# Two recurrent transformer layers: constant mask rows in the stacks, sequence 1's q and k inside the first maxima, and a reordered tail

## The chip, the cores and the metric

One core of a Trainium2 chip. The time is device microseconds of one execution. Before: 641.8 us, the median of 3 runs (640.47 to 642.42).

## The reference

Eight sequences of 512 tokens with 128 features pass two layers: `x = x + s * silu(g)`, with `xn` the layer norm of `x` in each.

- Layer 0, `s`: causal attention in latent form, 16 heads of 8. With `xn`, scores are `q_lat . c_kv / sqrt(8)`, masked above the diagonal, softmax, times values. Layer 0, `g`: a mixture of 8 experts (top 2; logits are `xn . w_route` plus the cosine of the token and the centroids), each a gelu network of 64 hidden units.
- Layer 1, `s`: a normed `h` gives keys and queries of 64 and values of 128; a matrix W is updated token after token, `W = W - 0.01 * (W k - v) k^T`, read out as `W q`; `s = xn + y`. Layer 1, `g`: `xn @ sign(weight).T`.

The sequential update is solved in four chunks of 128 tokens, each with the inverse of a triangular 128x128 matrix that is built up in levels.

## The kernel before

All engines walk one written schedule (`HEAD`, then `iteration` with `FIRST_PLAN`, `PLAN`, `LAST_PLAN`). An iteration has four groups of four heads, each of ten units; a unit (step, u) can carry named pieces, and every engine executes its own part of each piece in this order. In a steady iteration a unit does three things:

- `s_unit`, for the next sequence: TensorE makes scores of queries by keys in `ps_s` (units 0 to 3: four diagonal tiles of 128 columns and the mask as one matmul of 4x128 columns, identity times `negmask`; units 4 to 9: tiles off the diagonal). VectorE takes the maximum over keys into `cand` (L1422).
- `e_unit`, for the current sequence: scores again, transposed, in `ps_e` (first the mask on the diagonal tiles, then for each tile row j one matmul over all later queries), and ScalarE takes the exponential into `prob` (L1218). The maximum is already subtracted, since it stands as rows 72 to 74 of the stack.
- the pieces: `pv` (probabilities times values, L907), the experts (`h`, `gb`, `out`), and for older sequences the second layer (`c_...`, `lev_a1` to `lev_d6`, `c_u`, `c_y`, `c_r`).

`qst` and `kst` are the stacks, two of each by parity: q and k are split in three bf16 parts, and 9 part pairs x 8 features are 72 rows (PAIRS), with three rows of maxima in q against ones in k (SROWS = 75). They are filled through DRAM: SP writes the parts to `q_scratch` and `k_scratch` (L428), loads them back in halves of eight heads (L441, L443; `stacks0`, `stacks1`), and `m_rows` sends the maxima through `max_scratch` (L449, L451). All of these stand in SP's one queue, in the schedule's order; `e_unit` waits for `mrow_loaded`.

`HEAD` works through the weights, the layer norm, q and k of sequence 0, its router and experts, then q and k of sequence 1, its stacks, gelu and constants for the masks; the iteration under `FIRST_PLAN` then has only the maxima of sequence 0, with idle matmuls (`keep_busy`) in place of `e_unit`. Six iterations run `PLAN`, a seventh has no second sequence to load, and the last runs `LAST_PLAN`: exponentials of sequence 7 beside the second layer of sequence 6, then the tail, in which the second layers of 6 and 7 are interleaved (`last:` is sequence 7).

Token norms for the cosine come from squares on ScalarE (`squares_of`, L1166) and a power on GpSimd (`token_norms`). Layer norms: VectorE's statistics, GpSimd's power of -0.5 (`ln_rstd`), VectorE's scaling (`ln_norm`; `hn_norm` and `xn2_norm` in layer 1, whose two scalings are one power over eight values, L576).

## Time and profile before

| | |
|---|---|
| median of 3 runs | 641.8 us |
| profiled execution | 642.34 us |
| its span, first to last instruction | 640.6 us |
| mean granted clock of TensorE | 0.984 of full |
| TensorE / VectorE / ScalarE / GpSimd busy | 94% / 61% / 57% / 26% |
| bytes read from and written to DRAM | 24.46 and 9.96 MB |

Busy shares are averages over stages with different limits. Matmuls overlap, so a TensorE that counts as busy need not be streaming all the time. A "releaser" is what ended an idle time.

### The profile page before, as it was taken

The numbers are of one execution on the slowest core, as the hardware profiler recorded it, in microseconds if no ns is written. First come the engines' busy times: TensorE is split into PE (matmuls) and PEld (weight loads), VectorE is DVE, ScalarE is ACT, GpSimd is POOL, SyncE is SP. The second block draws the span as 40 slices with busy tenths as digits, with TensorE's granted clock in tenths as the row PEclk, the third lists the DMA queues.
The fourth block names the chain that finished last, engine by engine and source line by source line (L and its number), as shares of the span: only waits on it lengthen the run. The fifth ranks groups of instructions, "written<-read, shape, count | busy, mean of one in ns | idle before, by whom it ended". The sixth has DMA issues, their size and how long they took to land.

```text
span 640.6 us, 16904 instructions
## 1 busy us (share of the span) xinstructions
PE 601.3 (94%) x7002; PEld 382.2 (60%) x7002; DVE 390.7 (61%) x975; ACT 363.0 (57%) x743; POOL 163.4 (26%) x310
## 2 busy tenths in 40 slices
PE   7799999899999999999999999999999998997987
PEld 3345655576565766586566756586667665553564
DVE  3369676758668576848566675857675664413432
ACT  4331467755675575746674576646674667574420
POOL 4356122313223220332223230412232202210211
PEclk9899999999999999999999999999999999899888
DMA  3665003500341013310441014210430000100001
GB/s 85 162 157 135 9 1 99 141 9 4 87 121 56 4 35 99 92 41 9 107 110 42 2 52 112 62 41 11 124 92 27 3 10 1 42 1 1 4 2 33
DMA packets 28886, 35.60 MB, mean 56 GB/s; under 512 B 3947, under 2 KB 25258, under 8 KB 27658
## 3 DMA queue, kind: packets, MB, share of 16 engines
q1 hardware_dynamic: 28778, 34.52, 21.1%
q8 instruction: 55, 0.90, 0.6%
q14 instruction: 21, 0.17, 0.1%
q10 hardware_dynamic: 32, 0.01, 0.0%
HBM read 24.46 MB, written 9.96 MB: 54 GB/s over the span
## 4 chain that ended last, share of the span: by engine, by line
PE 60%; DVE 10%; issue 4%; ACT 4%; POOL 2%; DVEq 0%; POOLq 0%
PE ps_v L907 8%; PE ps_s L888 7%; PE ps_e L873 6%; PE ps_a L833 4%; PE ps_a L819 3%; PE ps_e L870 3%; DVE cand L1422 3%; PE ps_c L972 3%; PE ps_s L891 2%; PE ps_c L954 2%; PE ps_a L790 2%; PE ps_c L1057 2%; DVE stats L1344 1%; DVE hid L1406 1%; PE ps_c L941 1%
## 5 line engine op out<-in xcount | busy, mean ns | idle before, releaser
L1422 DVE TENSOR_REDUCE cand<-ps_s 128x4 f32<-128x512 f32 (+1 forms) x320 | 212.1, 684 | 63.7 <-PE ps_s L891 44.4
L1218 ACT ACTIVATE prob<-ps_e 128x512 f32<-128x512 f32 x320 | 188.8, 598 | 100.4 <-PE ps_e L873 96.4
L888 PE MATMUL ps_s<-kst,qst 72*128 72x128 bf16 (+1 forms) x1024 | 124.7, 233 | 8.9 <-DVE cand L1422 7.1
L873 PE MATMUL ps_e<-qst,kst 75*128 75x384 bf16 (+3 forms) x512 | 122.1, 300 | 0.0
L888 PEld LDWEIGHTS ps_s<-kst,qst 72*128 72x128 bf16 x1024 | 71.4, 98 | 69.3 <-DVE cand L1422 39.5
L907 PE MATMUL ps_v<-prob,vaug 128*32 128x512 f32 (+3 forms) x1024 | 89.5, 445 | 0.0
L870 PE MATMUL ps_e<-identb,negmask 128*128 128x256 bf16 (+1 forms) x320 | 81.0, 253 | 7.2 <-ACT prob L1218 7.0
L873 PEld LDWEIGHTS ps_e<-qst,kst 75*128 75x128 bf16 x512 | 50.3, 98 | 17.8 <-issue 0.3
L891 PE MATMUL ps_s<-negmask,identb 128*128 128x512 bf16 x128 | 48.8, 381 | 0.0
L706 PE MATMUL ps_e<-identb 128*128 128x512 bf16 x116 | 42.8, 427 | 3.1 <-POOL state L501 3.1
L870 PEld LDWEIGHTS ps_e<-identb,negmask 128*128 128x128 bf16 x320 | 31.3, 98 | 18.5 <-ACT prob L1218 14.4
L907 PEld LDWEIGHTS ps_v<-prob,vaug 128*32 128x32 f32 x1024 | 23.5, 108 | 30.2 <-issue 25.4
L972 PEld LDWEIGHTS ps_c<-second 32*32 32x32 f32 x2072 | 24.9, 107 | 23.0 <-issue 16.1
L819 PE MATMUL ps_a<-xnT,w1s 128*128 128x512 f32 x64 | 34.4, 619 | 2.9 <-DVE logit L1379 2.1
L617 POOL CAST mparts<-nm 128x32 bf16<-128x32 f32 x16 | 3.3, 209 | 126.3 <-DVE nm L1429 126.3
L972 PE MATMUL ps_c<-second 32*32 32x32 f32 x2072 | 32.6, 194 | 3.0 <-DVE second L1485 2.5
L833 PE MATMUL ps_a<-w2s,hid 128*128 128x128 f32 x256 | 32.7, 281 | 0.9 <-ACT mrow L1210 0.9
L1197 ACT ACTIVATE hid<-ps_a,vecT 128x512 f32<-128x512 f32 x32 | 22.0, 687 | 20.1 <-PE ps_a L819 20.1
L833 PEld LDWEIGHTS ps_a<-w2s,hid 128*128 128x128 f32 x256 | 31.4, 192 | 1.8 <-ACT mrow L1210 1.5
L1411 DVE SCALAR_TENSOR_TENSOR gate_out<-tG,ps_a 128x512 f32<-128x512 f32 x8 | 5.5, 689 | 34.9 <-ACT tG L1205 34.9
L1205 ACT ACTIVATE tG<-ps_a 128x512 f32<-128x512 f32 x8 | 4.8, 597 | 38.4 <-PE ps_a L835 38.4
L1406 DVE TENSOR_TENSOR hid<-hid,ps_a 128x512 f32<-128x512 f32 x32 | 21.6, 677 | 4.1 <-PE ps_a L826 4.1
(336 smaller groups left out, 922.7 us busy)
## 6 DMA issues: line engine op xcount, KB each, us to landing
qst<-q_scratch SPq DMA_DIRECT2D x48, 192.0 KB
kst<-k_scratch SPq DMA_DIRECT2D x16, 576.0 KB
q_scratch<-qparts SPq DMA_DIRECT2D x24, 128.0 KB, 2.3
k_scratch<-kparts SPq DMA_DIRECT2D x24, 128.0 KB, 2.3
x_res<-in_L_attn_x_dram SPq DMA_DIRECT2D x8, 256.0 KB, 2.8
xn<-in_L_attn_x_dram SPq DMA_DIRECT2D x7, 256.0 KB, 3.3
out_dram<-second SPq DMA_DIRECT2D x7, 256.0 KB, 2.5
max_scratch<-mrow SPq DMA_DIRECT2D x16, 96.0 KB, 1.7
```

The costliest lines, as they stand in the source:

```text
L706: mm(ps_e[:, 1, :].rearrange("p (a c) -> p a c", c=P), identb[:, :], bcast(identb[:, :], 1, 4), start=True, stop=True, skip_group_check=True)
L819: mm(ps_a[:, :], w1s[:, 2 * c:2 * c + 2, :].rearrange("p e f -> p (e f)"), xnT[b.parity][:, :], start=True, stop=True)\
L833: mm(ps_a[:, tok(i)], hid[:, c, tok(i)], w2s[:, c, :], start=(i == 0 and c == 0), stop=False, skip_group_check=True)
L870: mm(diag, negmask[:, :], bcast(identb[:, :], 1, len(todo)), start=True, stop=False, skip_group_check=True)
L873: last = mm(ps_e[:, bank, at:at + TOK - P * j], k[0:SROWS, hd, tok(j)], q[0:SROWS, hd, P * j:TOK], start=False, stop=True, skip_group_chec ...
L888: last = mm(ps_s[:, bank, w * n:w * (n + 1)], q[0:PAIRS, hd, tok(i)], k[0:PAIRS, hd, keys[0]:keys[1]], start=(n == 0), stop=True, skip_gro ...
L891: last = mm(ps_s[:, bank, :].rearrange("p (a c) -> p a c", a=GH), identb[:, :], bcast(negmask[:, :], 1, GH), start=False, stop=True, skip_ ...
L907: last = mm(ps_v[32 * hh:32 * hh + 32, P * j:TOK], vaug[:, j, head_of(grp, hh), :], prob[:, u, o:o + TOK - P * j], start=(j == 0 and grp % ...
L972: last = mm(bank[SQ * col:SQ * col + SQ, SQ * i:SQ * i + SQ], lhsT(row, col, i), rhs[SQ * row:SQ * row + SQ, i, :], start=True, stop=True, ...
L1218: af(prob[:, u, :], ps_e[:, u % 2, :], ACT.Exp).then_inc(S["e_emptied"], 1)
L1406: vec.tensor_tensor(hid[:, c, :], hid[:, c, :], ps_a[:, :], ALU.mult).then_inc(S["a_emptied"], 1)
L1422: vec.tensor_reduce(cand[:, i, h0:h0 + FILLS * (len(hds) - 1) + 1:FILLS, S_SLOT[u]], ps_s[:, u % 2, :].rearrange("p (a c) -> p a c", a=len ...
```

## The change

Masks: rows 75 to 127 of the stacks (53, `MROWS`) get constants: the first rows of the identity in q, of `negmask` in k. A diagonal tile that is contracted over all 128 rows so gets the mask of its first 53 queries or keys, and the mask matmul covers the other 75 columns. In `e_unit` a tile row's matmul is cut into the diagonal tile (128 rows) and the rest (75 rows). Rows 72 to 74 of q must be zero during the maxima, so each half of a stack load also writes zeros there. The constants are built on GpSimd in `prob` and loaded into each parity once (`load_pads`).

Transfers: q's stack rows in pieces of 1024 instead of 4096 bytes, k's in three transfers without broadcast; q and k writes of sequence 0 alternate; fewer transfers for the small loads, the first expert weights on a semaphore of their own.

Order: in `HEAD` h0 and h1 come before the logits; xnt, q, k and stacks of sequence 1 move into the first maxima, as do `masks`. Token norms are computed on GpSimd from the variance and rstd. `ln_rstd` of layer 1 first makes the four values that `hn_norm` needs, then the others. `LAST_PLAN`: `pv2`, `yt`, `x1` come sooner; sequence 7's `xn2_norm`, `c_xn2t`, `c_ffn` and `c_vk` stand earlier. Some numbers of `keep_busy` matmuls differ.

```diff
-STACK_DMAS, WRITE_DMAS = 4, 6
+STACK_DMAS, WRITE_DMAS = 7, 6
 PAIRS = PARTS * PARTS * HD
 MAXROW = 96
 SROWS = PAIRS + PARTS
+MROWS = 128 - SROWS
+EVEN = 48
...
-    (2, 8): ["c_ffn"], (2, 9): ["pv1"], (3, 2): ["pv2"], (3, 4): ["yt"], (3, 6): ["pv0"], (3, 9): ["pv1"], (4, 0): ["lev_a1"],
-    (4, 1): ["lev_d1"], (4, 2): ["pv2", "lev_a2"], (4, 3): ["yt", "x1", "last:ln2_stats", "lev_d2", "fill4", "last:ln2_rstd", "lev_a3", "last:hn_norm", "fill6"],
-    (4, 4): ["last:c_ht", "lev_d3", "fill2", "last:c_kt", "last:c_qt", "lev_a4", "fill1"],
-    (4, 5): ["last:c_gram", "lev_d4", "turned0", "low_blocks", "turned1", "last:c_vk", "fill1", "lev_a5", "fill2"],
-    (4, 6): ["last:lev_a1", "lev_d5", "fill1", "last:lev_d1", "lev_a6", "fill1", "last:xn2_norm"], (4, 7): ["last:lev_a2", "lev_d6", "fill1", "last:lev_d2", "c_u0", "fill1"],
-    (4, 8): ["last:lev_a3", "c_y0", "fill1", "last:lev_d3", "c_r1", "fill1"], (4, 9): ["last:lev_a4", "c_u1", "fill1", "last:lev_d4", "last:turned0", "last:low_blocks", "last:turned1", "c_y1", "fill1"],
-    (5, 0): ["last:c_xn2t", "c_r2", "fill1", "last:lev_a5", "c_u2", "last:c_ffn"], (5, 1): ["last:lev_d5", "prev:c_y2", "fill1", "last:lev_a6", "prev:c_r3", "fill1"],
-    (5, 2): ["last:lev_d6", "prev:c_u3", "prev:c_y3", "fill1", "last:c_u0", "prev:c_out", "fill1", "last:c_y0"],
-    (5, 4): ["last:c_r1", "fill1", "last:c_u1", "fill1", "last:c_y1"], (5, 5): ["last:c_r2", "fill1", "last:c_u2", "fill1", "last:c_y2"],
+    (2, 8): ["c_ffn"], (2, 9): ["pv1"], (3, 2): ["pv2"], (3, 4): ["yt"], (3, 6): ["pv0"], (3, 9): ["pv1"], (4, 0): ["pv2", "lev_a1", "fill2"],
+    (4, 1): ["yt", "x1", "last:ln2_stats", "lev_d1", "fill8", "lev_a2", "fill4", "last:ln2_rstd", "lev_d2", "fill2", "last:hn_norm", "lev_a3", "fill2"],
+    (4, 3): ["last:c_ht", "last:xn2_norm", "fill2", "last:c_kt", "last:c_qt", "lev_d3", "fill1", "last:c_vk", "last:c_gram", "lev_a4", "fill1"],
+    (4, 4): ["lev_d4", "last:c_xn2t", "lev_a5", "turned0", "low_blocks", "turned1", "fill1", "last:lev_a1", "last:c_ffn", "fill1", "last:lev_d1", "lev_d5", "fill1"],
+    (4, 5): ["last:lev_a2", "lev_a6", "fill1", "last:lev_d2", "lev_d6", "fill1", "last:lev_a3", "c_u0", "fill1"], (4, 6): ["last:lev_d3", "c_y0", "fill1"],
+    (4, 7): ["last:lev_a4", "c_r1", "fill1", "last:lev_d4", "c_u1", "fill1"], (4, 8): ["last:lev_a5", "last:turned0", "last:low_blocks", "last:turned1", "c_y1", "fill1"],
+    (4, 9): ["last:lev_d5", "c_r2", "fill1", "c_u2", "last:lev_a6"], (5, 0): ["prev:c_y2", "fill1", "last:lev_d6", "prev:c_r3", "fill1"],
+    (5, 2): ["last:c_u0", "prev:c_u3", "fill1", "last:c_y0", "prev:c_y3", "fill1"],
+    (5, 4): ["last:c_r1", "fill1", "prev:c_out", "last:c_u1", "fill1", "last:c_y1"], (5, 5): ["last:c_r2", "fill1", "last:c_u2", "fill1", "last:c_y2"],
...
-HEAD = [("weights", None), ("ln1_stats", 0), ("ln1_rstd", 0), ("centroids", None), ("ln1_norm", 0), ("ln1_stats", 1), ("ln1_rstd", 1),
-        ("xnt", 0), ("weight_k", None), ("q", 0), ("k", 0), ("stacks0", 0), ("stacks1", 0), ("rn_first", 0), ("constants", None),
-        ("late_loads", None), ("prepare", None), ("logits", 0), ("ln1_norm", 1), ("h0", 0), ("gates", 0), ("h1", 0), ("gate_norm", 0), ("h2", 0),
-        ("h3", 0), ("xnt", 1), ("q", 1), ("k", 1), ("stacks0", 1), ("stacks1", 1), ("gelu", 0), ("masks", None), ("busy", None)]
+HEAD = [("weights", None), ("ln1_stats", 0), ("ln1_rstd", 0), ("rn_first", 0), ("centroids", None), ("ln1_norm", 0), ("ln1_stats", 1), ("ln1_rstd", 1),
+        ("xnt", 0), ("weight_k", None), ("q", 0), ("k", 0), ("stacks0", 0), ("stacks1", 0), ("constants", None), ("late_loads", None),
+        ("prepare", None), ("h0", 0), ("h1", 0), ("logits", 0), ("h2", 0), ("gates", 0), ("ln1_norm", 1), ("h3", 0), ("gate_norm", 0),
+        ("gelu", 0), ("busy", None)]
 FIRST_PLAN = {
-    (0, 1): ["gt"], (0, 7): ["prepare2"], (0, 9): ["prepare3"], (1, 1): ["prepare4"],
-    (2, 0): ["m_parts0"], (2, 4): ["m_rows0"], (2, 5): ["masks2"], (3, 2): ["v"], (4, 0): ["m_parts1"],
+    (0, 0): ["xnt"], (0, 2): ["q"], (0, 4): ["k", "stacks0", "stacks1"], (0, 7): ["gt"], (1, 2): ["masks"], (1, 6): ["prepare2"], (1, 9): ["prepare3"],
+    (2, 0): ["m_parts0"], (2, 2): ["prepare4"], (2, 4): ["m_rows0"], (2, 5): ["masks2"], (3, 2): ["v"], (4, 0): ["m_parts1"],
 }
...
-    yield from iteration(None, seqs[0], None, None, None, plan=FIRST_PLAN)
+    yield from iteration(seqs[1], seqs[0], None, None, None, plan=FIRST_PLAN)
...
+        q_pad, k_pad = (prob[0:MROWS, 0, 256 * n:256 * n + 256].bitcast(BF16) for n in range(2))
...
+            def load_pads(p):
+
+                few = MROWS - EVEN
+                sp.wait_ge(S["pad_ready"], 2)
+                for st, pad in ((qst[p], q_pad), (kst[p], k_pad)):
+                    sp.dma_start(st[SROWS + few:P, :, :], bcast(pad[few:MROWS, :], 1, HEADS)).then_inc(S[f"pads_loaded{p}"], 16)
+                    sp.dma_start(st[SROWS:SROWS + few, :, :], bcast(pad[0:few, :], 1, HEADS)).then_inc(S[f"pads_loaded{p}"], 16)
+                sp.wait_ge(S["ones_ready"], 1)
+                sp.dma_start(kst[p][PAIRS:SROWS, :, :], bcast(ones_bf[:, :], 1, HEADS)).then_inc(S[f"pads_loaded{p}"], 16)
...
+            sp.dma_start(w1s[:, :, :], w1_in.rearrange("e d f -> d e f")).then_inc(S["expert_loaded"], 16)
+            load_pads(0)
...
+                if b.c == 0 and n == 0:
+                    return
+                tensors = (0, 1) if b.c == 0 else (n,)
                 for r, ready in enumerate(("hi_ready", "mid_ready", "parts_ready")):
-                    sp.wait_ge(S[ready], b.count(2, n + 1))
-                    to = (q_scratch[b.parity][:, r], k_scratch[b.parity][r])[n]
-                    sp.dma_start(to.rearrange("d h q -> h d q"), parts[n][:, r, :]).then_inc(S["scratch_written"], 16)
+                    for t in tensors:
+                        sp.wait_ge(S[ready], b.count(2, t + 1))
+                        to = (q_scratch[b.parity][:, r], k_scratch[b.parity][r])[t]
+                        sp.dma_start(to.rearrange("d h q -> h d q"), parts[t][:, r, :]).then_inc(S["scratch_written"], 16)
...
-                                 max_dma_last_dim=4096).then_inc(loaded, 16)
-                sp.dma_start(kst[b.parity][0:PAIRS, heads, :].rearrange("p h q -> p (h q)"), bcast(k_rows, 1, PARTS)).then_inc(loaded, 16)
+                                 max_dma_last_dim=1024).then_inc(loaded, 16)
+                sp.dma_start(qst[b.parity][PAIRS:SROWS, heads, :], bcast(zeros_bf[:, :], 1, HALF_HEADS)).then_inc(loaded, 16)
+                for r in range(PARTS):
+                    sp.dma_start(kst[b.parity][r:PAIRS:PARTS, heads, :].rearrange("p h q -> p (h q)"), k_rows,
+                                 max_dma_last_dim=1024).then_inc(loaded, 16)
...
+            for pad, of in ((q_pad, identb), (k_pad, negmask)):
+                g.tensor_copy(pad.rearrange("p (i c) -> p i c", c=P), bcast(of[0:MROWS, :], 1, NT)).then_inc(S["pad_ready"], 1)
...
-                g.tensor_scalar(r.vare[n][:, 0, :], variance, LN_EPS, None, ALU.add).then_inc(r.S[f"var{n}"], 1)
                 if n == 0:
+                    g.tensor_scalar(r.vare[n][:, 0, :], variance, LN_EPS, None, ALU.add).then_inc(S["var0"], 1)
                     pool.wait_ge(S["var0"], o.count(1, 1))
                     g.tensor_tensor(r.rstd[n][:, 0, :], r.vare[n][:, 0, :], halfpow[:, 0, :], ALU.pow).then_inc(S["rstd0"], 1)
+                    pool.wait_ge(S["rstd0"], o.count(1, 1))
+                    g.tensor_tensor(ss[:, :], variance, r.rstd[n][:, 0, :], ALU.mult).then_inc(S["ss_ready"], 1)
+                    pool.wait_ge(S["ss_ready"], o.count(2, 1))
+                    g.tensor_tensor(ss[:, :], ss[:, :], r.rstd[n][:, 0, :], ALU.mult).then_inc(S["ss_ready"], 1)
                 else:
                     g.tensor_scalar(r.vare[n][:, 1, :], variance, 1 + LN_EPS, LN_EPS * LN_EPS, ALU.mult, ALU.add).then_inc(r.S["var1"], 1)
+                    pool.wait_ge(r.S["var1"], o.count(2, 1))
+                    g.tensor_tensor(r.rstd[n][:, 1, :], r.vare[n][:, 1, :], halfpow[:, 0, :], ALU.pow).then_inc(r.S["rstd1"], 1)
+                    g.tensor_scalar(r.vare[n][:, 0, :], variance, LN_EPS, None, ALU.add).then_inc(r.S["var1"], 1)
                     pool.wait_ge(r.S["var1"], o.count(2, 2))
-                    g.tensor_tensor(r.rstd[n][:, :, :], r.vare[n][:, :, :], halfpow[:, :, :], ALU.pow).then_inc(r.S["rstd1"], 1)
+                    g.tensor_tensor(r.rstd[n][:, 0, :], r.vare[n][:, 0, :], halfpow[:, 0, :], ALU.pow).then_inc(r.S["rstd1"], 1)
...
-                    diag = ps_e[:, bank, 0:P].rearrange("p (a c) -> p a c", a=1)
+                    diag = ps_e[:, bank, MROWS:P].rearrange("p (a c) -> p a c", a=1)
                 else:
                     step = 384 if u < 8 else 256
-                    diag = ps_e[:, bank, :].rearrange("p (a c) -> p a c", c=P)[:, 0:step // P + 1:step // P, :]
-                mm(diag, negmask[:, :], bcast(identb[:, :], 1, len(todo)), start=True, stop=False, skip_group_check=True)
+                    diag = ps_e[:, bank, :].rearrange("p (a c) -> p a c", c=P)[:, 0:step // P + 1:step // P, MROWS:P]
+                mm(diag, negmask[:, :], bcast(identb[:, MROWS:P], 1, len(todo)), start=True, stop=False, skip_group_check=True)
                 for hh, j, at in todo:
                     hd = head_of(grp, hh)
-                    last = mm(ps_e[:, bank, at:at + TOK - P * j], k[0:SROWS, hd, tok(j)], q[0:SROWS, hd, P * j:TOK],
+                    last = mm(ps_e[:, bank, at:at + P], k[:, hd, tok(j)], q[:, hd, tok(j)],
                               start=False, stop=True, skip_group_check=True)
+                    if j < NT - 1:
+                        last = mm(ps_e[:, bank, at + P:at + TOK - P * j], k[0:SROWS, hd, tok(j)], q[0:SROWS, hd, P * (j + 1):TOK],
+                                  start=False, stop=True, skip_group_check=True)
...
+                if b.c < 2 and grp == 0 and u == 0:
+                    pe.wait_ge(S[f"pads_loaded{b.parity}"], 80)
+                rows = P if u < NT else PAIRS
                 for n, hh in enumerate(hds):
                     w = keys[1] - keys[0]
                     hd = head_of(grp, hh)
-                    last = mm(ps_s[:, bank, w * n:w * (n + 1)], q[0:PAIRS, hd, tok(i)], k[0:PAIRS, hd, keys[0]:keys[1]],
+                    last = mm(ps_s[:, bank, w * n:w * (n + 1)], q[0:rows, hd, tok(i)], k[0:rows, hd, keys[0]:keys[1]],
                               start=(n == 0), stop=True, skip_group_check=True)
                 if u < NT:
-                    last = mm(ps_s[:, bank, :].rearrange("p (a c) -> p a c", a=GH), identb[:, :], bcast(negmask[:, :], 1, GH),
+                    last = mm(ps_s[:, bank, :].rearrange("p (a c) -> p a c", a=GH)[:, :, MROWS:P], identb[:, :],
+                              bcast(negmask[:, MROWS:P], 1, GH),
...
-            def squares_of(b):
-                after(act, S["rn_ready"], b.count(1, 0))
-                for i in range(NT):
-                    af(tG[:, i * P:(i + 1) * P], x_tile(b)[:, i, :], ACT.Square, accum_out=ss[:, i:i + 1]).then_inc(S["ss_ready"], 1)
```

Left out: GpSimd's setup in another order (identity first; `negmask`, a row block of zeros and the pads before the rest), `token_norms` reading `ss` scaled by 128, and the changed numbers of `keep_busy`.

## Rows read from the trace of the kernel before

**Rows 1.** The page: busy time, share of the span and instructions of each engine.

```profile
PE 601.3 (94%) x7002; PEld 382.2 (60%) x7002; DVE 390.7 (61%) x975; ACT 363.0 (57%) x743; POOL 163.4 (26%) x310
```

**Rows 2.** Windows by stage: PE, PEld, DVE, ACT, POOL busy, clock, DMA share, GB/s.

```profile
0.00:36.04 36.04, 27.93 (x91) 12.27 (x92) 11.88 (x51) 14.70 (x42) 15.57 (x40) 0.95 0.53 131
...
36.04:65.40 29.36, 28.96 (x216) 14.94 (x215) 25.60 (x43) 6.55 (x16) 15.42 (x45) 1.00 0.57 133
...
65.40:121.00 55.60, 53.20 (x481) 32.05 (x478) 38.02 (x82) 36.42 (x67) 11.46 (x26) 1.00 0.22 56
...
262.40:333.20 70.80, 68.63 (x859) 45.65 (x858) 47.93 (x121) 44.55 (x91) 18.35 (x32) 1.00 0.23 61
...
542.80:584.70 41.90, 38.02 (x310) 21.51 (x314) 10.62 (x29) 28.26 (x55) 8.52 (x13) 0.96 0.06 16
...
584.70:640.60 55.90, 45.80 (x795) 30.05 (x787) 22.52 (x71) 12.76 (x38) 9.42 (x11) 0.88 0.04 11
```

**Rows 3.** Windows, two stretches inside one steady stage.

```profile
261.60:273.40 11.80, 10.27 (x87) 5.77 (x85) 11.73 (x30) 7.19 (x13) 5.39 (x8) 1.00 0.14 39
...
296.00:304.30 8.30, 8.24 (x195) 5.46 (x194) 8.16 (x26) 6.03 (x15) 2.14 (x6) 1.00 0.05 16
```

**Rows 4.** TensorE instructions in order of time, one unit: start, length, line, operation.

```profile
275.48 0.39 PE L888 MATMUL ps_s<-kst,qst 72*128 72x128 bf16 x4
275.71 0.38 PE L891 MATMUL ps_s<-negmask,identb 128*128 128x512 bf16 x1
275.93 0.22 PE L870 MATMUL ps_e<-identb,negmask 128*128 128x128 bf16 x1
275.98 0.38 PE L873 MATMUL ps_e<-qst,kst 75*128 75x512 bf16 x1
```

**Rows 5.** Groups by line and shape: busy us, mean ns, idle before.

```profile
L870 PE MATMUL ps_e<-identb,negmask 128*128 128x256 bf16 x192 | 53.0, 276 | 1.4 <-ACT prob L1218 1.4
...
L891 PE MATMUL ps_s<-negmask,identb 128*128 128x512 bf16 x128 | 48.8, 381 | 0.0
...
L873 PEld LDWEIGHTS ps_e<-qst,kst 75*128 75x128 bf16 x512 | 50.3, 98 | 17.8 <-issue 0.3
```

**Rows 6.** Transfers issued by SP, in order of time.

```profile
54.73 0.34 SPq L449 DMA_DIRECT2D max_scratch<-mrow  x1
...
59.98 0.24 SPq L451 DMA_DIRECT2D qst<-max_scratch  x1
...
243.84 1.13 SPq L441 DMA_DIRECT2D qst<-q_scratch  x3
```

**Rows 7.** VectorE instructions in order of time.

```profile
260.52 0.69 DVE L1422 TENSOR_REDUCE cand<-ps_s 128x4 f32<-128x512 f32 x1
...
587.02 0.69 DVE L1435 COPY yT<-ps_v 128x512 f32<-128x512 f32 x1
...
594.42 1.11 DVE L1359 TENSOR_SCALAR qst<-x,last_mv,last_rstd 128x128 f32<-128x128 f32 x4 [1.85 <-POOL last_rstd L576]
```

**Rows 8.** TensorE in order of time, in the start and in the tail.

```profile
28.78 0.66 PE L778 MATMUL ps_a<-ident,att 128*128 128x128 f32 x4 [0.78 <-ACT hid L1197]
...
613.76 0.45 PE L972 MATMUL ps_s<-qst 32*32 32x32 f32 x32
...
616.87 0.44 PE L972 MATMUL ps_s<-qst 32*32 32x32 f32 x16 [0.30 <-ACT kst L1229]
...
620.03 0.81 PE L972 MATMUL ps_s<-qst 32*32 32x32 f32 x24 [1.41 <-DVE kst L1512]
```

**Rows 9.** Windows, the first maxima while the stacks are loaded.

```profile
42.00:60.00 18.00, 17.96 (x137) 9.34 (x136) 15.99 (x26) 1.86 (x7) 6.67 (x26) 1.00 0.64 138
```

**Rows 10.** GpSimd's powers in order of time: four values, then eight.

```profile
5.47 1.04 POOL L572 TENSOR_TENSOR rstd<-vare,halfpow 128x4 f32<-128x4 f32 x1
...
592.72 1.67 POOL L576 TENSOR_TENSOR last_rstd<-last_vare,halfpow 128x8 f32<-128x8 f32 x1
```

**Rows 11.** Windows, a stretch of the tail.

```profile
620.20:630.40 10.20, 9.82 (x62) 6.93 (x59) 2.84 (x8) 0.90 (x3) 3.93 (x4) 0.50 0.00 0
```

73 lines of the change are left out of this document (36 added, 37 removed).

## The prediction

> **What bounds the kernel now.** I read the page first, then busy time by stage, then one steady stage cut into stretches, then single matmuls in order of time, and last the start and the tail.
>
> TensorE is busy for 601.3 of 640.6 us [rows 1]. "Busy" overstates it, since matmuls overlap, so look at the stages [rows 2]: the start to the first maximum (36.0 us), the maxima of sequence 0 (29.4), then seven stages that put the maxima of one sequence beside the exponentials of another (55.6, five of 70.8, and one of 68.0, which together end at 542.8), the exponentials of sequence 7 alone (41.9), and the tail (55.9). In a steady stage TensorE is busy for 68.6 of 70.8 us, VectorE for 47.9 and ScalarE for 44.6: TensorE sets the pace on average. But in two stretches of that stage VectorE is busy for 11.73 of 11.80 us and for 8.16 of 8.30 [rows 3]. There the maxima and the work between them set the pace, and a shorter matmul only makes TensorE wait. 20.1 of 70.8 us are such, so what is saved on TensorE comes through for about two thirds. In the first maxima VectorE has 25.6 of 29.4 us, one reduction after another (40 in that time, 0.73 us each); in the last exponentials stage nobody is full.
>
> **The mask part.** For the spacing of matmuls, look at start times, not at durations [rows 4]. The four S matmuls of 128 columns start within 275.48 to 275.71, so 0.057 us each; the S mask of 512 columns holds the engine from 275.71 to 275.93, 0.22; the E mask of 128 columns 0.05. All of it is about 0.43 ns per column, at a granted clock of 1.00.
>
> S: each of 128 masks [rows 5] shrinks from 4 x 128 to 4 x 75 columns: 212 x 0.43 = 0.09 us, times 16 per sequence = 1.45 us per stage. E: 64 diagonal tiles per sequence lose 53 columns each, in 16 masks of one tile and 24 of two (192 over the run [rows 5]): 64 x 53 x 0.43 = 1.45 us. Against that the E matmul of tiles 0 to 2 is cut in two (48 more weight loads and matmuls per sequence, columns in all the same). What a cut costs no row shows; the distance from column time is 2 to 3 ns in these rows, so 0.1 us per stage. Below: 0, the load hides completely. Above: a weight load is recorded with 98 ns [rows 5], against 55 for the 128 columns before it: 43 ns x 48 = 2.1 us. I take 0.1, since the four S matmuls each bring such a load and still start 0.057 apart. A mask of 75 columns is shorter than any bf16 matmul here; if loads need the 55 ns, 16 x 0.02 = 0.35 us is lost. The contraction over 128 rows instead of 72 or 75 I price at nothing: the identity masks already use 128 rows and have the same price per column.
>
> Sum per stage: 1.45 + 1.45 - 0.1 = 2.8 us on TensorE. About 0.9 of it lies in VectorE's two stretches (groups 0 and 2, most units of each). Of the other 1.9 I take 1.6 as real, because the second layer's chains go TensorE to ScalarE to TensorE and TensorE waits a little more. Six stages of 1.6 and the first (55.6 us, fewer other pieces, so more of it is back-to-back maxima) with 1.3: **10.9 us**. Bounds: 0.5 per stage (3.5) and all of it (19.6).
>
> The Trainium skill, "TensorE: Matmul & The Clock Gate", section "Back-to-back issue gap", speaks against the cut: in a stream of load and matmul pairs it gives about 81 ns per matmul of 128 columns, so 48 more pairs would cost far more than I allow. By that figure a stage would pay 48 x 28 ns = 1.3 us more, and the seven stages about 6 us of gain less. This trace has 0.057 us for just such pairs, and the measurement decides.
>
> Squares for the token norms leave ScalarE; two small GpSimd operations replace them behind the rstd. In the body both lie under TensorE: nothing.
>
> **Stack loads.** Each half issues seven transfers instead of four (q in 1 KB pieces, k in three, a zero row block). Three q issues take 1.13 us of SP's time at 243.84 [rows 6]; the half is needed 16.7 us later, when the next stage's maxima begin at 260.52 [rows 7]. Seven at 0.4 to 0.8 us are 3 to 6 us, so they are hidden: nothing. Queued behind them on SP are only m_rows1, the residual and the next x. If the cover went, each us late would cost a us in each stage.
>
> **The start.** Before, sequence 1's transposes, q and k stand between sequence 0's feed-forward and the maxima: from 28.78 [rows 8] to the first maximum at 36.04, 7.3 us. They move into the first maxima. Then the stack load is what comes last. Its issue time hardly moves: SP now passes five pad transfers and their wait on GpSimd (pads built behind two more memsets), but the parts are the later event; q and k writes alternate, about 1 us saved. I expect the first maximum at about 28.5. The moved work costs in the first maxima: two subtractions over 128x512 out of PSUM, which I price like a reduction of that size, 0.69 us [rows 7], plus waits because q passes TensorE, ScalarE, VectorE while only a few reductions are there to cover: 2.5 to 3 us. So the maxima would end 7.5 - 2.7 = 4.8 us sooner.
>
> What is late next is the queue of transfers. In order after 21 us: stacks of sequence 0 (2.3 MB), late weights 0.3, the second pads (2 x 53 rows x 16 KB = 1.7), parts 0.8, stacks of sequence 1 (2.3), together 7.4 MB. The first exponential also waits for m_rows0, whose second transfer is issued only when the first has landed: before, at 59.98 against 54.73 for the first [rows 6], i.e. behind the stacks. In 42 to 60 us the engines moved 138 GB/s at a share of 0.64 [rows 9], so 216 at a full share. 7.4 MB at 180 to 216 GB/s from 21 us end at 55 to 62, plus two landings of about 2 us that the queue cannot cover, so the exponentials start at 60 to 66 instead of 65.4. I take 62.3: **3.1 us** won, bounds 0 and 5.
>
> **Last exponentials (41.9 us).** Only the E masks: 1.3 us on TensorE, but ScalarE and TensorE alternate there. The first layer-norm power before hn_norm takes four values, not eight. I take **1 us**; bounds 0 and 2.
>
> **The tail.** (a) pv2 moves ahead of the level pieces, so VectorE's copy of yT, 587.02 before [rows 7], starts about 1.3 us sooner. (b) The rstd chain: eight-value power 1.67 us [rows 10], four-value power 1.04 [rows 10], one tensor_scalar less before it: 0.9 us. Of these 2.2 us part is taken back, since lev_d2 of sequence 6 now stands in front of hn_norm on VectorE: hn_norm, 594.42 before, at about 593.2. (c) c_xn2t and c_ffn of sequence 7 move ahead. Before, lev_d4 starts at 613.76, lev_a5 at 616.87, released by c_xn2t's copy, and lev_d5 at 620.03, released by c_ffn's product [rows 8]: 6.3 us from d4 to d5. Now lev_a5 can follow d4 after about 1.3 us and d5 after 2.5, so 3.8 less. The same work must fit in earlier, where TensorE is full (PE groups of sequences 6 and 7 interleave): 1.5 us back, and xn2_norm 1.1 on VectorE. From this: about 1.2 + 3.8 - 2 = 3.0. (d) Before, 620.2 to 630.4 ran at a granted clock of 0.50, the 1.2 GHz level [rows 11], after a stretch in which TensorE waited. With the wait gone part of it may go; busy there 9.8 us, worth up to 4. I count 1. Tail: **4 us**; bounds 0 and 8.
>
> Sum: 3.1 + 10.9 + 1 + 4 = 19 us from the profiled execution's 642.3 (span 640.6 and 1.7 around it), so 623.3. The median, 641.8, is 0.5 lower: I say **623**.
>
> **Rivals.**
> - *The gain stays behind VectorE.* Stretches of 99% load grow once TensorE is faster, as rows 3 let one fear; against it, VectorE has 23 us spare per stage. 0.5 instead of 1.6 per stage: 623 + 7 = 630 (to 634). Chance 0.19.
> - *A floor per weight load.* 98 ns per pair rather than 55: E loses 2.1 us per stage and gains 1.1 to 1.45, only S remains: about 0.6 per stage, 1 us less in each of seven, and 630. Against it the 0.057 us spacing. Chance 0.08. The skill's 81 ns lies between.
> - *More comes through*: full mask saving and no clock drop in the tail, 607 to 614. For it: 1.9 us lie outside VectorE's stretches for certain. Chance 0.14.
> - *The start and the tail give nothing* (transfers of the pads, the earlier gate work in the way): 623 + 7 = 630. Chance 0.04.
> - *Slower: SP's issues.* If 1 KB pieces make an issue four times as long (1.5 us for q, 3 for k), the seven take 14 us and the half lands about 4 us late at the start of every stage: 7 x 4 = 28, so 651. It decides from 2.7 us late per stage, where seven stages eat the 19. Nothing speaks for it but that no such piece size is loaded here before. Chance 0.03.
>
> My forecast (616 to 628 by its own terms) has 0.52. The range that leaves out two in ten is 611 to 633. A measurement here cannot tell less than 0.3%, 2 us, from no change: faster 0.95, same 0.02, slower 0.03.
>
> **What would show it.** The spacing of the 75-column masks (33 or 55 ns; S masks 0.13 us), the cut matmuls starting 55 ns apart; stage length near 69.2; VectorE still full in the same stretches; first maximum near 28.5 and first exponential near 62, released by m_rows; hn_norm near 1.2 us sooner relative to the last exponential; lev_d5 of sequence 7 within 3 us of lev_d4; less of the slow clock after it. Wrong would be: a stage at 70.8 (VectorE or chains), maxima that wait for a stack load, or a longer start.

## The result and the profile after

Five runs of the changed kernel gave 647.5 us (median) and six of the one before 640.5, ratio 1.009 [1.007, 1.012]. A sixth execution of the changed kernel, at a mean granted clock of 0.555, took 905.6 us and is in no comparison. A second comparison, with ten and thirteen runs, gave 645.0 against 642.4, ratio 1.003 [1.001, 1.006]. So the change made the kernel a little slower, by 0.3 to 0.9%, where 623 us was forecast. The profile below is an execution of the second comparison: span 644.3 us.

The page of the changed kernel, busy time by engine; TensorE has 20 us less to do than before [rows 1], VectorE as much:

```profile
PE 581.6 (90%) x7385; PEld 393.3 (61%) x7385; DVE 390.9 (61%) x975; ACT 352.5 (55%) x679; POOL 172.0 (27%) x337
```

Its windows by stage, with the columns of [rows 2]: the start to the first row maximum, from there to the first exponential, and a steady stage.

```profile
0.00:39.23 39.23, 23.97 (x74) 10.75 (x75) 10.56 (x48) 10.54 (x23) 14.80 (x43) 0.83 0.75 137
39.23:84.37 45.14, 30.73 (x225) 16.46 (x224) 27.40 (x45) 8.51 (x19) 19.99 (x53) 0.87 0.80 148
277.04:346.34 69.30, 66.32 (x907) 47.05 (x906) 47.85 (x122) 43.26 (x84) 19.37 (x35) 1.00 0.27 62
```

A steady stage takes 69.3 us instead of 70.8: as forecast. But the first exponential comes at 84.4 us instead of 65.4. What the change wins behind that point, it has lost by then. In the stretch before it TensorE is busy for 30.7 of 45.1 us and the DMA engines at a share of 0.80.

What holds the start is read from SP's issues, in order of time (start, length of the issue, what is moved); `prob` is the tile in which GpSimd built the pads:

```profile
7.24 2.87 SPq L411 DMA_DIRECT2D kst<-prob  x1
...
13.22 2.70 SPq L414 DMA_DIRECT2D kst<-ones_bf  x1
...
23.42 0.60 SPq L448 DMA_DIRECT2D q_scratch<-qparts  x1
...
29.03 1.20 SPq L462 DMA_DIRECT2D qst<-q_scratch  x3
...
44.34 3.06 SPq L411 DMA_DIRECT2D kst<-prob  x1
...
50.45 2.67 SPq L414 DMA_DIRECT2D kst<-ones_bf  x1
53.17 4.33 SPq L448 DMA_DIRECT2D q_scratch<-qparts  x3
...
73.60 0.50 SPq L473 DMA_DIRECT2D max_scratch<-mrow  x1
81.32 0.26 SPq L475 DMA_DIRECT2D qst<-max_scratch  x1
```

The issues of the k pads and of the row of ones last 2.7 to 3.1 us each, where those of the two q pads before them last 0.75 and 0.91 and most small loads 0.25 to 0.6. The length isn't that of the transfer: the ones are 48 KB, and without pads in front of them (run 3) their issue takes 0.93 us. So I read it as SP waiting until the queue takes more. The small loads behind them are issued by 23.4, the parts are written from there on, and the stacks of sequence 0 are issued at 29.0; before the change the same issue stood at 20.6. The second set holds SP from 42.7 to 53.1, and sequence 1's parts and stacks come behind it. The last of the stacks is issued at 73.6; m_rows0 follows, and its second transfer at 81.3.

TensorE in order of time shows who waits for this: first for the small loads, then for the stack of sequence 1, then for the maxima's row.

```profile
25.68 0.27 PE L761 MATMUL ps_c<-ident,vecs 8*128 8x8 f32 x1 [11.87 <-DMA vkrow<-in_L_attn_bk_dram]
```

```profile
74.00 0.58 PE L925 MATMUL ps_s<-kst,qst 128*128 128x128 bf16 x4 [3.17 <-DMA kst<-k_scratch]
...
83.66 0.25 PE L901 MATMUL ps_e<-identb,negmask 128*128 128x75 bf16 x1 [8.82 <-DMA qst<-max_scratch]
```

ScalarE has its first exponential behind that, after 15.7 us without work:

```profile
84.37 0.60 ACT L1247 ACTIVATE prob<-ps_e 128x512 f32<-128x512 f32 x1 [15.71 <-PE ps_e L907]
```

### The profile page after: what moved, and what is told of

Same layout as the page of the kernel before. It is cut to its first block, busy times and chain, and to the rows that moved or that the text cites. A ratio compares the mean times of both kernels' runs of the same rounds, so it can differ in the third digit from the quotient of the medians.

```text
span 903.9 us, 17696 instructions
## 1 busy us (share of the span) xinstructions
PE 885.7 (98%) x7385; PEld 559.3 (62%) x7385; DVE 400.4 (44%) x975; ACT 361.7 (40%) x679; POOL 171.9 (19%) x337
## 4 chain that ended last, share of the span: by engine, by line
PE 94%; DVE 3%; SPq 2%; ACT 1%; issue 0%; POOL 0%; DMA 0%; POOLq 0%; DVEq 0%
PE ps_v L945 14%; PE ps_s L925 13%; PE ps_e L907 8%; PE ps_a L850 6%; PE ps_a L864 5%; PE ps_e L904 5%; PE ps_e L738 4%; PE ps_c L1010 4%; PE ps_e L901 3%; PE ps_s L928 3%; PE ps_a L819 3%; PE ps_c L992 2%; PE ps_a L828 1%; PE ps_c L1095 1%; PE ps_c L1070 1%; PE ps_v L955 1%
## 5 line engine op out<-in xcount | busy, mean ns | idle before, releaser
L925 PE MATMUL ps_s<-kst,qst 128*128 128x128 bf16 (+2 forms) x1024 | 176.9, 304 | 0.9 <-DVE cand L1453 0.5
L925 PEld LDWEIGHTS ps_s<-kst,qst 72*128 72x128 bf16 (+1 forms) x1024 | 97.8, 119 | 98.4 <-issue 51.3
L904 PE MATMUL ps_e<-qst,kst 128*128 128x128 bf16 x512 | 141.8, 297 | 0.0
L907 PE MATMUL ps_e<-qst,kst 75*128 75x256 bf16 (+2 forms) x384 | 139.5, 381 | 0.0
L945 PE MATMUL ps_v<-prob,vaug 128*32 128x512 f32 (+3 forms) x1024 | 136.7, 649 | 0.0
L901 PE MATMUL ps_e<-identb,negmask 128*128 128x150 bf16 (+1 forms) x320 | 90.7, 284 | 0.8 <-ACT prob L1247 0.7
L904 PEld LDWEIGHTS ps_e<-qst,kst 128*128 128x128 bf16 x512 | 63.4, 124 | 22.3 <-issue 1.2
L850 PE MATMUL ps_a<-xnT,w1s 128*128 128x512 f32 x64 | 55.7, 983 | 1.3 <-ACT hid L1226 0.8
L864 PE MATMUL ps_a<-w2s,hid 128*128 128x128 f32 x256 | 53.4, 384 | 0.3 <-ACT mrow L1239 0.3
L928 PE MATMUL ps_s<-negmask,identb 128*128 128x300 bf16 x128 | 53.3, 416 | 0.0
L1010 PEld LDWEIGHTS ps_c<-second 32*32 32x32 f32 x2072 | 29.8, 124 | 30.6 <-issue 28.1
```

Of the source, the lines that this page charges most:

```text
L850: mm(ps_a[:, :], w1s[:, 2 * c:2 * c + 2, :].rearrange("p e f -> p (e f)"), xnT[b.parity][:, :], start=True, stop=True)\
L864: mm(ps_a[:, tok(i)], hid[:, c, tok(i)], w2s[:, c, :], start=(i == 0 and c == 0), stop=False, skip_group_check=True)
L901: mm(diag, negmask[:, :], bcast(identb[:, MROWS:P], 1, len(todo)), start=True, stop=False, skip_group_check=True)
L904: last = mm(ps_e[:, bank, at:at + P], k[:, hd, tok(j)], q[:, hd, tok(j)], start=False, stop=True, skip_group_check=True)
L907: last = mm(ps_e[:, bank, at + P:at + TOK - P * j], k[0:SROWS, hd, tok(j)], q[0:SROWS, hd, P * (j + 1):TOK], start=False, stop=True, skip_ ...
L925: last = mm(ps_s[:, bank, w * n:w * (n + 1)], q[0:rows, hd, tok(i)], k[0:rows, hd, keys[0]:keys[1]], start=(n == 0), stop=True, skip_group ...
```

## Experiments

In all of them "the changed kernel" is the kernel after the change. Runs 1 to 4, 5 to 8 and 9 to 12 were each measured beside the kernel before, which took 642.4, 642.5 and 641.3 us; ratios are to it. "By the spans" compares one profiled execution of each kernel, which a difference in the start can shift by 2 us (see run 8).

**1. The changed kernel again.**

> The changed kernel once more, for a profile at the full granted clock. Theory Q (queue): the pad transfers fill SP's queue, the five issues take up to 3 us each, the small loads behind them land near 20 us, and TensorE stands still in the start for about 9 us; the masks themselves save 1.3 to 1.9 us per steady stage as forecast. Then the first maximum is at 37 to 38 us and a steady stage has 69 us. Theory C (clock): the start is not late by much, but TensorE gets the lower clock in more stretches of the body; then a steady stage has 71 us or more and stretches at 0.5 stand in it. Time in both: 645 to 648.

Measured: 645.0 us, ratio 1.003 [1.001, 1.006]. The trace is the one shown above: the first maximum at 39.2 us, 11.9 us of idle TensorE in front of 25.7, a steady stage of 69.3. Theory Q, with a start that is 1 to 2 us later still. It is the base of the next three.

**2. The mask matmuls of before in the changed kernel**, the pads still loaded but read by nobody.

```diff
-rows = P if u < NT else PAIRS          # and 75-column masks, cut E matmuls
+rows = PAIRS                           # 512-column S mask, 128-column E masks, E matmul in one
```

> Both kinds of mask as before (full mask matmuls over all columns, 72 and 75 rows, E matmul not cut); pads still loaded, though unused. Theory Q: slower than the changed kernel by what the masks save, 9 to 13 us, so 655 to 660, with the same late start. Theory C: the 128-row matmuls cost the clock, so this one is as fast as the changed kernel or faster, 640 to 646.

Measured: 659.2 us, ratio 1.025 [1.017, 1.034]; steady stages are back at 70.7 us: theory Q. TensorE's program still waits for the pads, but the trace puts its long waits in the start down to the small loads (13.9 us), sequence 1's stack (1.6) and the maxima's row (9.2), not to them. The masks win 14 us by the medians, 11 by the spans (655.4 to 644.3).

**3. The same without the four pad transfers of each parity.** The row of ones is still loaded.

```diff
-for st, pad in ((qst[p], q_pad), (kst[p], k_pad)):
-    sp.dma_start(st[SROWS + few:P, :, :], ...)
-    sp.dma_start(st[SROWS:SROWS + few, :, :], ...)
```

> As e1, and the four pad transfers of each parity are gone too. Theory Q: the small loads land by 15 us, the first maximum comes at 28 to 30 us, and the whole is 8 to 12 us faster than e1: 645 to 650. Theory C: the pads are hidden and this equals e1 within 2 us.

Measured: 632.1 us, ratio 0.984 [0.979, 0.990]. The eight transfers cost 27 us by the medians and 23.6 by the spans (655.4 to 631.8), in a kernel that doesn't even use them. The first maximum comes at 28.1 instead of 38.8 us, the first exponential at 63.4 instead of 83.0. Theory Q in kind, but its size was missed by more than half: it allowed 8 to 12 us, for the first maximum alone, and left out that the second set stands ahead of sequence 1's stacks. Run 7 takes the two sets apart.

**4. The last iteration's plan of before.**

```diff
-LAST_PLAN = { ... (4, 0): ["pv2", "lev_a1", "fill2"], ... }
+LAST_PLAN = { ... (4, 0): ["lev_a1"], ... }                # the table before the change
```

> The changed kernel with the old order of the last iteration (LAST_PLAN). If the new tail saves the 4 us that were forecast, this is 3 to 5 us slower than the changed kernel, about 650. If the tail's clock or order spoiled it (rival), it is equal or faster: 640 to 646.

Measured: 651.2 us, ratio 1.013 [1.007, 1.018]. By the medians the new plan wins 6 us, by the spans (648.0 to 644.3) 3.7, and of that only 0.5 lies behind the last row maximum; in the rest the two starts differ, which the plan doesn't touch. So this pair sizes the plan badly, and run 11 does it again on a quieter base.

**5. The pads kept and used, but loaded when the queue is idle.** In run 3's trace the DMA share between 70 and 90 us is 0.01 to 0.05. The pads get tiles of their own (`prob` is in use by then), sequences 0 and 1 use the masks of before, the other six the constant rows.

```diff
-q_pad, k_pad = (prob[0:MROWS, 0, ...].bitcast(BF16) for n in range(2))
+q_pad, k_pad = (sb(name, [MROWS, TOK], BF16) for name in ("q_pad", "k_pad"))
 def load_x(b):
     ...
+    if b.c == 2:
+        load_pads(0)
 def m_rows(b, half):
     ...
+    if (b.c, half) == (0, 1):
+        load_pads(1)
-rows = P if u < NT else PAIRS
+rows = P if u < NT and b.c >= 2 else PAIRS     # the E masks and cuts likewise
```

> The changed kernel with the pad rows kept, but in tiles of their own and loaded later: the four pad transfers of parity 0 are issued behind the load of sequence 2's x (about 61 us), those of parity 1 behind sequence 0's second row maxima (about 76 us), where the trace of the run without pads shows a DMA share of 0.01 to 0.05; the first two sequences use the mask matmuls of before, the six others the constant rows. Theory A, that the pads cost time only because they stand in the queue in front of the start's loads: the start is that of the run without pads (632.1 us), the stages from sequence 2 on take 69.4 instead of 70.7 us, so 632 less 9 to 11, about 622 us, ratio about 0.968. Rival B, that the pads cost wherever they are, since they hold SP for about 12 us per parity and the transfers behind them: the row maxima's transfers come late and the exponentials with them, and 628 to 636 us results. Rival C, that the masks' saving seen so far (14 us by medians) belongs to the start and not to the stages: 630 us.

Measured: 622.6 us, ratio 0.970 [0.965, 0.974]; theory A. It is the fastest kernel of the study together with run 9, 3% below the kernel before. SP's issues of the first set in it, and the windows of the start and of the 12 us in which that set moves:

```profile
58.57 0.65 SPq L411 DMA_DIRECT2D qst<-q_pad  x1
...
60.11 3.79 SPq L411 DMA_DIRECT2D kst<-k_pad  x1
64.33 2.29 SPq L412 DMA_DIRECT2D kst<-k_pad  x1
```

```profile
0.00:21.00 21.00, 16.38 (x57) 7.20 (x57) 10.09 (x44) 8.05 (x20) 14.00 (x39) 1.00 0.47 122
21.00:61.20 40.20, 36.07 (x240) 19.09 (x241) 27.84 (x49) 10.96 (x24) 19.18 (x52) 0.96 0.74 156
61.00:73.00 12.00, 11.55 (x109) 6.95 (x108) 9.94 (x16) 7.45 (x13) 2.22 (x6) 1.00 1.08 129
```

The pads are as slow here as at the start: issues of 3.8 and 2.3 us, 129 GB/s at a share of 1.08, so 12 us and more in which the queue does nothing else. But nothing waits behind them. In the windows of the changed kernel, the same two stretches:

```profile
0.00:21.00 21.00, 11.87 (x33) 5.21 (x33) 5.60 (x23) 5.38 (x12) 13.67 (x39) 0.92 0.81 127
21.00:84.40 63.40, 42.86 (x264) 22.04 (x265) 32.36 (x70) 13.70 (x30) 21.12 (x57) 0.82 0.77 149
```

Rate times time gives what is moved before the first exponential: 8.8 MB in the kernel with late pads, 12.1 MB in the changed one. The 3.3 MB between them are close to the two sets (1.7 MB each). The mean rate up to there is nearly the same in both, 145 and 143 GB/s, so the time goes with the bytes: the first exponentials are 84.4 - 61.2 = 23.2 us apart. There is a second way to be late in this, SP's own wait at each issue. No run issues the pads from another engine, so what that wait adds to the transfers' own time isn't shown.

**6. The first set issued behind the small loads.**

```diff
-load_pads(0)
 sp.wait_ge(S["small_zeroed"], 1)
 for dst, src in zero_loads + loads:
     sp.dma_start(dst, src).then_inc(S["loaded"], 16)
+load_pads(0)
```

> The changed kernel with the first five pad transfers issued behind the small loads (vectors, second weights, value and key rows) instead of in front of them; nothing is left out. Theory A, that the transfers' volume fills the start: the small loads' wait (11.9 us of idle TensorE before 25.7 us) goes, but the parts and the stacks still stand behind the pads, the first maximum stays at 37 to 40 us, and the time is 641 to 646 us. Rival B, that the order alone cost, since the preparation waits for the small loads: the first maximum comes at 30 us or so and the time is 633 to 637 us.

Measured: 645.0 us, ratio 1.004 [1.001, 1.007], as without the edit (645.0). The small loads are now issued by 10.1 us instead of 23.4 and their wait is gone, yet the first maximum stays at 39.3 and the first exponential comes at 86.6. TensorE now waits the longer for the stack:

```profile
38.31 0.61 PE L925 MATMUL ps_s<-kst,qst 128*128 128x128 bf16 x4 [12.98 <-DMA kst<-k_scratch]
```

Whether the pads stand before or behind the small loads isn't the cause; that they pass ahead of the stacks is.

**7. Only the second set loaded**, with the masks of before (between runs 2 and 3).

```diff
-for st, pad in ((qst[p], q_pad), (kst[p], k_pad)):
+for st, pad in ((qst[p], q_pad), (kst[p], k_pad)) if p else ():
```

> The changed kernel with the mask matmuls of before and without the four pad transfers of parity 0 (its ones are loaded); those of parity 1 stay where they are, behind the late weights. The same with both sets took 659 us, with neither 632 us. Theory A, that both sets cost, the first by the late first maximum (38.8 against 28.1 us), the second by sequence 1's stacks and the first row maxima, which stand behind them: about 10 to 12 us come back, 646 to 649 us. Rival B, that only the first set costs and the second is hidden: 632 to 635 us. Rival C, that only the second costs, since the first maxima of sequence 0 end into a wait for row maxima anyway: 656 to 659 us.

Measured: 647.3 us, ratio 1.008 [1.004, 1.012]: theory A. Of the 27 us between runs 2 and 3 the first set has 12 and the second 15 by the medians; by the spans (655.4, 643.7, 631.8) each has 12. Its windows to the first maximum and on to the first exponential at 72.4:

```profile
0.00:29.86 29.86, 20.69 (x73) 9.26 (x74) 10.84 (x49) 12.27 (x23) 15.14 (x43) 0.97 0.56 126
29.86:72.36 42.50, 33.70 (x224) 17.79 (x223) 27.72 (x45) 6.86 (x18) 20.07 (x53) 0.90 0.76 152
```

In the three kernels that differ in nothing but the sets, the first exponential comes at 63.4 us with none ahead of it, at 72.4 with one and at 83.0 with two. With what the following stage adds, a set of 1.7 MB costs about 12 us by the spans.

**8. The stack loads of before** in run 3's kernel.

```diff
-for s in range(PARTS): ... q_rows, max_dma_last_dim=1024
-sp.dma_start(qst[b.parity][PAIRS:SROWS, heads, :], bcast(zeros_bf[:, :], 1, HALF_HEADS))
-for r in range(PARTS): ... k_rows, max_dma_last_dim=1024
+for s in range(PARTS): ... q_rows, max_dma_last_dim=4096
+sp.dma_start(kst[b.parity][0:PAIRS, heads, :]..., bcast(k_rows, 1, PARTS))
```

> The kernel with the mask matmuls of before and no pads (632.1 us), with the stack loads as before the change too: per half three loads of 4096-element pieces and one broadcast instead of seven loads in 1024-element pieces. Theory A (the prediction's step), that the extra issues of SP cost nothing: 631 to 633 us. Rival B, that the seven issues hold the queue at the start, where the row maxima's second transfer was issued 7 us behind the stacks: 626 to 630 us. Rival C, that the smaller pieces move faster: 634 to 638 us without them.

Measured: 628.7 us, ratio 0.979 [0.975, 0.984], 3.4 us less than run 3 with intervals that overlap; by the spans 2.1. The number lies in rival B's range. 1.8 of the 2.1 lie ahead of the second maxima (61.6 against 63.3 us), half of them ahead of the first. The steady stages are equal to 0.1 us. Look at the granted clock before believing rival B: in run 3's execution it is at the 1.2 GHz level in more of the first maxima.

```profile
26.00:34.00 8.00, 7.07 (x33) 4.27 (x34) 2.08 (x3) 1.37 (x3) 0.00 (x0) 0.57 0.88 163
```

```profile
26.00:34.00 8.00, 7.22 (x38) 4.06 (x39) 3.83 (x6) 1.64 (x3) 0.91 (x2) 0.79 0.73 165
```

The first line is run 3 (clock 0.57), the second this run (0.79). The kernel of run 5, with seven issues, has 0.79 there too and its second maxima at 61.1 us.

**9. The same edit on the kernel with late pads**, with one load of zeros kept.

> The kernel with late pads (622.6 us) with the stack loads of before the change again, and one load of zeros beside them: five per half instead of seven, in pieces of 4096 elements. Without pads the same edit took the time from 632.1 to 628.7 us. Theory A, that it is the seven issues at the start that cost: 3 us less again, 619 to 620.5 us. Rival B, that the two effects share their cover: 622 to 623 us.

Measured: 621.3 us, ratio 0.968 [0.965, 0.971], against 0.970 [0.965, 0.974]; the spans are 620.0 and 619.8. 621.3 lies between the two ranges, but the traces are alike: second maxima at 61.3 and 61.1 us, the clock at 0.79 from 26 to 34 us in both. Here the form of the stack loads makes no difference (rival B), so run 8's 3 us are no price of the seven issues. Runs 5 and 12 have the same program up to 61 us and show 0.79 and 0.57 in that stretch, so the clock there differs between executions without an edit. That it is what parts run 8 from run 3 fits, but wasn't tested by itself. Run 9 also keeps the zeros that run 8 drops.

**10. The pads in pieces of 4 KB.** They are built four heads wide and moved with a quarter of the pieces.

```diff
-sp.dma_start(st[SROWS + few:P, :, :], bcast(pad[few:MROWS, :], 1, HEADS))
+sp.dma_start(wide(st[SROWS + few:P, :, :]), bcast(pad[few:MROWS, :], 1, HEADS // 4))
```

> The changed kernel with its pads where they are, but built four heads wide, so that their transfers go in pieces of 4 KB instead of 1 KB (the same bytes, a quarter of the pieces); their build on POOL grows by some 2 us each and may delay the first of them as much. Nothing is left out. In the kernel with late pads, two of the four moved 1.7 MB per parity at 129 GB/s and a DMA share of 1.08. Theory A, that a piece has a price of its own: the pads go at 180 GB/s or more, and of the 24 us that they cost a third or more comes back, 632 to 638 us. Rival B, that the price is per byte, or at the writing side: 643 to 649 us.

Measured: 645.9 us, ratio 1.007 [1.004, 1.009]: no gain, rival B. The pads are issued 2.6 us later (8.05 instead of 5.49, for the longer build) and the issues of the k pads last 2.76 and 2.77 us, much as before (2.87 and 3.02). The price isn't one of the pieces. Whether it goes with the bytes, or with the 53 partitions that are read and written, run 13 tells.

**11. The plan of before for the last iteration, with late pads.**

> The kernel with late pads (622.6 us) with the last iteration's plan as before the change. In the changed kernel the same edit cost 6.2 us by the medians, but only 0.4 to 1 us of it lay behind the last row maxima in the two profiled executions, the rest in the start. Theory A (the prediction's step: pv2 and yt earlier 1.3, c_xn2t and c_ffn earlier 1.8): 625 to 629 us. Rival B, that the difference was the start's: 622 to 624 us.

Measured: 624.2 us, ratio 0.975 [0.969, 0.980], so the plan is worth 1.6 us by the medians, which were measured beside different runs of the kernel before, and 3.2 by the ratios and by the spans (623.0 to 619.8), of which 2.7 lie behind the last exponentials. The median falls between the two ranges and the intervals overlap; the traces speak for theory A. TensorE in order of time, the last levels of sequence 7: with the plan of before and with the new one.

```profile
599.82 0.72 PE L1022 MATMUL ps_s<-qst 32*32 32x32 f32 x32
...
606.35 0.59 PE L1022 MATMUL ps_s<-qst 32*32 32x32 f32 x24 [1.41 <-DVE kst L1555]
```

```profile
600.57 0.45 PE L1022 MATMUL ps_s<-qst 32*32 32x32 f32 x32
...
602.81 0.59 PE L1022 MATMUL ps_s<-qst 32*32 32x32 f32 x24
```

The waits behind lev_d4 that [rows 8] shows are back with the old plan (6.5 us from d4 to d5) and gone with the new one (2.2).

**12. The row maxima's masks of before, with late pads.** The exponentials' masks stay changed.

```diff
-rows = P if u < NT and b.c >= 2 else PAIRS
-cut = 0 if b.c < 2 else MROWS
+rows = PAIRS
+cut = 0
```

> The kernel with late pads (622.6 us) with the row maxima's masks as before the change in all sequences (the masks of the exponentials stay changed). The masks' saving in a steady stage was 1.45 us of 70.8 where TensorE lost 2.8 us of work. Theory A, that TensorE and VectorE share the stages' limit, so that each kind of mask gives about half: 0.7 us per stage, 4 to 5 us in all, 626.5 to 628 us. Rival B, that the row maxima wait for VectorE anyway and only the exponentials' masks count: 622 to 623.5 us. Rival C, that only the maxima's masks count: 630 to 632 us.

Measured: 629.2 us, ratio 0.980 [0.976, 0.984]. One steady stage in this kernel and in the one with late pads:

```profile
257.97:328.16 70.19, 67.70 (x907) 47.05 (x906) 47.90 (x122) 43.38 (x83) 19.40 (x35) 1.00 0.26 63
```

```profile
253.93:323.21 69.28, 66.30 (x907) 47.05 (x906) 47.85 (x121) 43.27 (x84) 19.40 (x35) 1.00 0.26 64
```

TensorE is busy 1.4 us longer, as forecast for the S masks; 0.9 us of it shows in the stage, where VectorE and ScalarE do the same in both. The E masks have the other 0.5 of some 1.4. From sequence 2's first row maximum to sequence 7's last it makes 5.3 us; that the medians are 6.7 apart and the spans 8.8 has to do with the start, which is 2.4 us later in this execution and which the edit doesn't reach (its clock is 0.57 from 26 to 34 us, as in run 3, and not 0.79). The median lies outside all three ranges. By the stages it is theory A, with more for S than for E.

**13. The transfers alone.** A kernel of SP's transfers only, in eight groups of four, each group waited for before the next; its output is a copy of the input. It was executed once.

```diff
+go([(t[80:128, :, :], bcast(src[5:53, 0:W], HEADS)) for t in tiles])        # as the pads go
+go([(t[40:88, :, :], bcast(src[5:53, 0:W], HEADS)) for t in tiles])
+go([(t[0:48, :, :], bcast(src[5:53, 0:W], HEADS)) for t in tiles])
+go([(t[40:88, :, :], bcast(src[40:88, 0:W], HEADS)) for t in tiles])
+...
```

> Transfers alone, the rest of the work left out (the output is a copy of the input). Eight groups one after the other, each of four transfers of 768 KB (48 rows of 16 KB, the shape of a large pad transfer; in the last group 128 rows of 6 KB): from partitions 5 to 52 to partitions 80 to 127, as the pads go; to 40 to 87; to 0 to 47; from 40 to 87 to 40 to 87; to 80 to 127 in pieces of 4 KB; from DRAM to 80 to 127 and to 40 to 87; from and to all 128 partitions. In the kernels the pads moved at 129 GB/s. Theory A, that the destination limits them, 48 neighbouring partitions in the upper half: the first group has about 129 GB/s (6 us per transfer), 40 to 87 a third more or better, and all 128 partitions 200 GB/s or more. Theory B, that reading the same piece from SBUF sixteen times limits them: the four groups within SBUF are equal at about 129, and DRAM to the same rows is faster. Theory C, that the engines give no more for pieces of 1 KB: all groups with such pieces are within 15% of each other, the 4 KB pieces faster.

Windows within the groups, in their order (the second group falls into two stretches; columns: GpSimd busy, clock, DMA share, GB/s):

```profile
4.00:25.00 21.00, 0.00 (x0) 1.00 1.07 143
29.00:40.00 11.00, 0.00 (x0) 1.00 0.92 188
40.00:51.00 11.00, 0.00 (x0) 1.00 0.52 97
53.00:75.00 22.00, 0.00 (x0) 1.00 1.02 140
78.00:92.00 14.00, 0.00 (x0) 1.00 0.92 218
94.00:116.00 22.00, 0.00 (x0) 1.00 0.98 141
119.00:141.00 22.00, 0.00 (x0) 1.00 1.02 142
144.00:157.00 13.00, 0.00 (x0) 1.00 0.96 236
160.00:170.00 10.00, 0.00 (x0) 1.00 0.95 314
```

No theory alone. From the first issue to the last landing the eight groups take 25.5, 23.6, 25.7, 15.9, 24.7, 25.7, 15.7 and 11.0 us. Theory A missed its own test: with 5 to 52 as the source, 40 to 87 as the destination is hardly faster than 80 to 127: 23.6 us instead of 25.5 (188 GB/s first, 97 after that, 142 over both windows). But 40 to 87 takes 218 GB/s from 40 to 87 and 236 from DRAM, so in that group it was the side that is read that set the rate. And 80 to 127 takes 142 from DRAM as well, so there the side that is written is enough. Theory B fails by that, and theory C by 218 against 143 for pieces of 1 KB; pieces of 4 KB give 141. All 128 partitions take 314. So the rate goes by which partitions a transfer touches at either end, and the DMA share doesn't show it: it is 1.02 at 142 and 0.95 at 314 GB/s. For 0 to 47 as a destination the run shows nothing, since its source was 5 to 52.

The Trainium skill, "SBUF — State Buffer", section "Door 1: The DMA port swizzle (why `[64,N]` ≈ `[32,N]`)", says that partitions 0 to 63 share one half of 16 ports and 64 to 127 the other, with partitions 32 apart on the same port. By that rule 80 to 127 lie on eight ports, four of them with eight rows and four with four, and 40 to 87 on twelve ports with four rows each. These runs agree in the order of the rates, if the fullest port at either end decides; the factor between the two is 1.5 to 1.7 here and not 2.

## Why the prediction was wrong, step by step

**The step that failed is the start: "Its issue time hardly moves: SP now passes five pad transfers and their wait on GpSimd ..., but the parts are the later event".** The stacks are issued at 29.0 us instead of 20.6. The parts were not the later event, because the five transfers take SP from 5.5 to 15.9 us, and the small loads and the parts' writes come behind. I priced the wait on GpSimd and not the queue: an issue costs 0.3 to 0.9 us only while the queue has room. Run 3 shows what the start is without them: first maximum 28.1 us, where 28.5 was forecast. Run 6 shows that it doesn't help to let the small loads pass first, since the first set's 1.7 MB still come ahead of the stacks; run 5 shows what does.

**The same volume is missing in the sum of the queue.** The prediction counted 7.4 MB from 21 us on, with the second set and without the first, at "180 to 216 GB/s", which came from scaling 138 GB/s by the share of 0.64 [rows 9]. Such scaling does not hold: at a share of 0.80 the changed kernel moved 148 GB/s (its windows above), at 1.08 the pads alone moved 129, and run 13 has full shares at anything from 140 to 314. In the changed kernel 9.4 MB went from 21 us to the first exponential, at 149 GB/s, and that is 63.4 us. So 2.0 MB were missing in the sum (13 us at that rate), and the 7.4 that it had take 50 us instead of the 34 to 41 that it allowed. 149 GB/s could have been read from the trace before the change, from 21 to 65.4 us:

```profile
21.00:65.40 44.40, 41.88 (x260) 19.87 (x259) 28.31 (x54) 13.97 (x33) 19.11 (x52) 0.98 0.64 149
```

Up to the first exponential the mean rate is 145 and 141 GB/s in runs 5 and 7 too, with no set and with one. The prediction's own bound, that the start gives nothing, stood at 65.4 us; the start in truth lost 19.

**What followed from it.** TensorE was busy for 0.8 of the 9 us from 74 to 83 us, and from there to 89 us its granted clock was still 0.50, so that the first matmuls of the exponentials ran at the 1.2 GHz level. The rival "the start and the tail give nothing (transfers of the pads ... in the way)" named the mechanism but bounded it at 7 us, with a chance of 0.04; it was 19 us at the first exponential, and the pads cost 27 us by the medians between runs 2 and 3. The other slow rival, SP's issues in the steady stages, did not come: the seven issues of a half take 4.4 us, and runs 5 and 9 have equal spans with seven and with five.

**What was right, by the kernel with late pads.** Its time, 622.6 us, is the forecast's 623. That it is so close is in part luck, since it is another kernel (two sequences keep the old masks) and its terms miss in both directions, as the list shows:

- *Masks.* In the changed kernel one S unit and a pair of E units, TensorE in order of time:

```profile
38.61 0.39 PE L925 MATMUL ps_s<-kst,qst 128*128 128x128 bf16 x4
38.83 0.29 PE L928 MATMUL ps_s<-negmask,identb 128*128 128x300 bf16 x1
38.96 0.38 PE L738 MATMUL ps_e<-identb 128*128 128x512 bf16 x1
```

```profile
89.67 0.23 PE L901 MATMUL ps_e<-identb,negmask 128*128 128x150 bf16 x1
89.74 0.22 PE L904 MATMUL ps_e<-qst,kst 128*128 128x128 bf16 x1
89.79 0.27 PE L907 MATMUL ps_e<-qst,kst 75*128 75x256 bf16 x1
89.90 0.22 PE L904 MATMUL ps_e<-qst,kst 128*128 128x128 bf16 x1
```

  The S mask holds the engine for 0.13 us (38.83 to 38.96), two masks of 75 columns for 0.07, and the cut matmuls of 128 columns for 0.05 to 0.06. There is no floor per weight load, as forecast from [rows 4]; the Trainium skill's 81 ns ("TensorE: Matmul & The Clock Gate", section "Back-to-back issue gap") are not met here either. In a steady stage TensorE is busy for 66.3 instead of 68.6 us (2.3 less, 2.8 forecast), and about 1.45 come through, where 1.6 was taken. VectorE's two full stretches of [rows 3] are still there, in the changed kernel:

```profile
278.10:290.50 12.40, 10.65 (x100) 6.25 (x98) 11.61 (x30) 7.89 (x14) 6.67 (x10) 1.00 0.21 56
311.50:320.00 8.50, 8.25 (x207) 5.85 (x204) 8.05 (x26) 6.28 (x13) 2.54 (x8) 1.00 0.05 14
```

  They keep the rest. Follow one row maximum, the last of the first stretch, before and in the changed kernel:

```profile
272.70 0.68 DVE L1422 TENSOR_REDUCE cand<-ps_s 128x4 f32<-128x512 f32 x1
```

```profile
289.05 0.69 DVE L1453 TENSOR_REDUCE cand<-ps_s 128x4 f32<-128x512 f32 x1
```

  It stands 12.18 us behind the stage's first maximum before (260.52) and 12.01 after (277.04), so only 0.17 us is won there. The second stretch wins 0.11, and the other 1.2 of the 1.5 us lie outside the two, as the prediction argued.

- *Q and k inside the first maxima.* From the first maximum of sequence 0 to the end of its last it is 28.8 us before, 32.1 in the changed kernel and 33.9 in the one with late pads: 3.3 and 5.0 more, where 2.7 was taken.
- *The start without pads.* The first maximum comes at 26.8 us (9.2 sooner; 7.5 was taken) and waits 2.1 us for the stack, so the stack load does come last. Less the 5.0, the maxima end 4.2 us sooner, and 4.8 was forecast. The first exponential, at 61.2 us, follows them at once (62.3 forecast), 4.2 sooner than before; 3.1 was taken, because the queue was expected to hold it. In this kernel it doesn't: `m_rows0`'s second transfer is issued at 57.3, and no wait for a transfer stands in front of the first `ps_e` matmul. The time was right there and the reason wasn't.
- *The tail.* VectorE's first norm of sequence 7 stands 10.3 us behind the start of ScalarE's last group of exponentials:

```profile
593.38 1.76 ACT L1247 ACTIVATE prob<-ps_e 128x512 f32<-128x512 f32 x3 [0.80 <-PE ps_e L904]
```

```profile
603.70 2.10 DVE L1390 TENSOR_SCALAR qst<-x,last_mv,last_rstd 128x128 f32<-128x128 f32 x8
```

  The last group before the change:

```profile
582.91 1.79 ACT L1218 ACTIVATE prob<-ps_e 128x512 f32<-128x512 f32 x3 [0.83 <-PE ps_e L873]
```

  Before it was 11.5 (594.42 [rows 7] less 582.91), so 1.2 sooner, as forecast. With the plan of before but the new order of the powers it is 10.5: 1.0 of it is the powers'. From that norm to lev_d5 it is 23.5 us instead of 25.6, 2.1 less, where 1.8 was taken. Behind lev_d5 it is 17.0 instead of 20.6 us, since the stretch at a clock of 0.50 [rows 11] is gone; I counted 1 for it, it was 3.6. But it is gone in run 11 too, with the plan of before (the last 16 us there run at a clock of 1.00), so the waits in front of it were not what brought it, or not alone. That stays open. Executions of the kernel before differ among themselves, from 639.0 us at a mean clock of 0.995 to 645.7 at 0.981, so part of the 3.6 may be the execution's.

Against the kernel before, the spans add up: 3.7 at the start of sequence 2's maxima, 7.2 in five steady stages (1.3 to 1.5 each) and 1.8 in the last one, 8.1 behind the last row maximum with the last exponentials' masks and the tail; 640.6 - 619.8 = 20.8 us, where the forecast had 19. Term by term: start 3.7 (3.1 forecast), masks 9.0 in six stages (10.9 in seven), last exponentials and tail 8.1 (5). The tail's surplus, most of it the clock, makes up for the stage without new masks.

## What to carry to other kernels

Constant data that is loaded only once still has to pass through the queue, and a start that already waits for transfers pays for each megabyte in full: here a set of 1.7 MB cost about 12 us with the small loads behind it or in front of it, and no cost of it shows when it was moved to a time with an idle queue. Sum the bytes ahead of the first dependent instruction, those issued before the stretch that one looks at too, and take the rate from a stretch of the same trace in which the same partitions are filled, not one scaled up by the share. An SP issue's length in a quiet trace is no price for it in a full queue. And when two executions of nearly the same kernel differ by 2 us, compare the granted clock of the same stretch before giving the difference to the edit.

## What the runs showed of the hardware

The issue of a pad transfer on SP took 0.65 to 0.9 us for the first two in most runs and 2.3 to 3.8 for the next ones, at the start and in an idle queue alike; in run 7 the second of them already took 3.6 and the next two 1.1 and 2.0. A load of 48 KB took 2.7 us behind them and 0.93 alone. It isn't the bytes under way alone that make the issue wait: in run 13 four transfers of the same 768 KB from DRAM, in pieces of 16 KB, were issued in 0.4 to 0.96 us each, while of the four that went as the pads go the third and fourth took 3.0 and 3.3. A transfer's rate went by the partitions at both of its ends: 140 to 143 GB/s where either end was 48 partitions on one side of 64, 218 to 236 where every end in SBUF was 40 to 87, 314 for all 128, with DMA shares of 0.92 to 1.07 in all windows but the second half of the group from 5 to 52 to 40 to 87 (0.52 at 97 GB/s); pieces of 4 KB gave what pieces of 1 KB did. Matmuls that contract over 128 rows instead of 72 cost TensorE nothing: the four S matmuls of 128 columns still start within 0.22 us.
